# A state space block written as 16 steps a unit: most of the unit's side work put at other steps, a fifth product on GpSimd

## The reference, cut to what matters

```python
x = x + mamba(layernorm_over_channels(x))          # pixel_shuffle: sequence of 1 + 2304, width 128
t = tokens(x)
t = t + ffn(layernorm(t))                          # ffn keeps its input but for tokens 1..128
```

```python
u, z = split(seq @ in_proj.T); u = silu(conv4(u) + conv_b)
dt, B, C = split(u @ x_proj.T); dt = softplus(dt @ dt_proj.T + dt_b)
h[n] = exp(dt * A[n]) * h[n] + (dt * u) * B[n]      # a scan over time, for each state n
y = (sum_n h[n] * C[n] + u * D) * silu(z);  out = y @ out_proj.T
```

## Time and profile before

| | |
|---|---|
| median of 3 runs | 1246.59 us (1246.4 to 1247.64) |
| the profiled execution's own time | 1246.36 us |
| its span | 1244.6 us |
| granted TensorE clock, mean | 0.943 |
| busy | PE 86%, DVE 88%, POOL 82%, ACT 70% |
| units 1 to 20 | 972.7 us, 48.64 us each |

### The profile page before, as it was taken

The page is one execution under the profiler, slowest core; times in us unless marked ns, Lnnn a source line. Parts: engine busy times, 40 slices in busy tenths (PEclk is TensorE's granted clock), DMA queues, the critical chain, the costliest instruction groups (busy, mean ns, idle before and its releaser), DMA issues.

```text
span 1244.6 us, 13235 instructions
## 1 busy us (share of the span) xinstructions
PE 1064.5 (86%) x3786; PEld 635.6 (51%) x3786; DVE 1089.3 (88%) x1220; ACT 870.6 (70%) x1581; POOL 1024.0 (82%) x679
## 2 busy tenths in 40 slices
PE   6688998988898888989987988998899898887997
PEld 4345555555455455555554554554555455443454
DVE  2898999898999989999989899989899998878684
ACT  4687687676777775876767777758767767657653
POOL 4598988978889879889889798898898897858674
PEclk9899999899999999999989999989999989988899
DMA  7222223222222221222221322212222322334351
GB/s 179 93 102 78 84 83 104 83 84 86 75 103 77 90 95 68 87 99 85 83 104 57 103 84 84 103 59 108 78 84 83 103 80 90 102 115 164 107 179 28
DMA packets 64538, 116.79 MB, mean 94 GB/s; under 512 B 34218, under 2 KB 47954, under 8 KB 64466
## 3 DMA queue, kind: packets, MB, share of 16 engines
q1 hardware_dynamic: 64466, 115.96, 27.4%
HBM read 108.47 MB, written 7.47 MB: 93 GB/s over the span
## 4 chain that ended last, share of the span: by engine, by line
ACT 33%; PE 32%; DVE 23%; issue 10%; POOL 2%; DVEq 0%; DMA 0%; POOLq 0%; ACTq 0%; SPq 0%
PE Yp L785 15%; DVE SCAN L1111 13%; ACT DA L513 6%; DVE SCAN L1076 5%; PE PP L797 3%; PE PP L810 3%; PE PP L866 2%; ACT L541 2%; ACT L529 2%; ACT UDT L535 2%; DVE GATES L1157 2%; POOL SCAN L448 2%; DVE VV L1087 2%; ACT DAS L521 2%; PE PP L818 2%
## 5 line engine op out<-in xcount | busy, mean ns | idle before, releaser
L448 POOL TENSOR_TENSOR SCAN<-SCAN,CS 128x768 f32<-128x768 f32 x384 | 692.4, 1817 | 121.7 <-DVE SCAN L1111 120.6
L1111 DVE TENSOR_TENSOR_SCAN SCAN<-DA,CAR,SCAN 128x384 f32<-128x384 f32 x672 | 638.8, 1002 | 54.6 <-ACT DA L513 54.6
L785 PE MATMUL Yp<-SCAN,IDENT 128*128 128x384 f32 x1536 | 597.7, 516 | 72.4 <-DVE VV L1087 70.9
L513 ACT ACTIVATE DA<-UDT,A 128x384 f32<-128x384 f32 x672 | 377.9, 578 | 257.0 <-DVE SCAN L1111 256.9
L785 PEld LDWEIGHTS Yp<-SCAN,IDENT 128*128 128x128 f32 x1536 | 297.0, 201 | 260.4 <-POOL SCAN L448 89.3
L1076 DVE TENSOR_TENSOR SCAN<-UDT,BB 128x768 f32<-128x768 f32 x240 | 224.9, 937 | 19.8 <-PE BB L767 19.7
L456 POOL TENSOR_TENSOR SCAN<-UDT,BS 128x768 f32<-128x768 f32 x96 | 173.9, 1812 | 0.0
L926 PE MATMUL PP<-XN,WT 128*128 128x384 f32 x352 | 124.4, 486 | 1.4 <-ACT ZB L626 1.4
L767 PE MATMUL BB<-PT,SEL 96*128 96x384 bf16 x288 | 98.2, 341 | 7.4 <-DVE DA L1076 4.4
L926 PEld LDWEIGHTS PP<-XN,WT 128*128 128x128 f32 x352 | 66.6, 189 | 48.5 <-issue 1.9
L468 POOL TENSOR_TENSOR UDT<-UDT 128x768 f32<-128x768 f32 x23 | 41.7, 1814 | 52.7 <-DVE UDT L1161 52.7
(11 more groups left out here) (212 smaller groups left out, 1233.9 us busy)
## 6 DMA issues: line engine op xcount, KB each, us to landing
CS<-bc_rows SPq DMA_DIRECT2D x96, 768.0 KB, 4.0
BS<-bc_rows SPq DMA_DIRECT2D x24, 768.0 KB, 6.1
out<-XN SPq DMA_DIRECT2D x32, 192.0 KB, 2.5
X<-in_x SPq DMA_DIRECT2D x24, 192.0 KB, 3.6
X<-in_L_ffn_memory_tokens SPq DMA_DIRECT2D x16, 256.0 KB, 2.9
XN<-in_L_ffn_memory_tokens SPq DMA_DIRECT2D x16, 256.0 KB, 3.0
bc_rows<-XDT SPq DMA_DIRECT2D x24, 48.0 KB, 1.5
X<-in_L_ffn_memory_router SPq DMA_DIRECT2D x1, 512.0 KB, 4.3
```

Source lines behind the costliest of these rows:

```text
L448: pool.tensor_tensor(M[:, n1 % MRING], HB[:, n1 % HRING], over_halves(CS[:, n1 % CRING]), ALU.mult).then_inc(m_ready, 1)
L513: act.activation(DA[:, h, 0:T], DT[:, par, h], ACT.Exp, scale=A[:, h, n:n + 1])\
L785: last = pe.matmul(Yp[:, h, 0:T], IDENT[:, :], M[:, n3 % MRING, h], start=n3 == 0, stop=n3 == NS - 1)
L1111: dve.tensor_tensor_scan(HB[:, s % HRING, h], factor, term, CAR[:, ds(J * NS * HALVES + s * HALVES + h, 1)], ALU.mult, ALU.add).then_inc(s ...
```

## The change

No arithmetic changes. The product with B of state 11 goes from VectorE to GpSimd, `AHEAD` becomes states 14 and 15, whose factors are made at steps 10 and 11 of the same unit, and the side work is hung on other steps. With the steps on which the pieces stand on their main engines:

| piece | before | after |
|---|---|---|
| Silu of U and of z, with two table loads (ACT) | 0, for J+1 and J-1 | 13, for J+2 and J |
| x projection (PE), copies of its rows (ACT) | 3, 4, for J+1 | 14, 15, for J+2 |
| parts: `LESS` (PE) | 4, 5 | 15 (of the unit before), 0 |
| dt projection (PE), Abs and Relu (ACT) | 7, 7 | 2, 2 |
| rest of softplus (ACT), last two pieces (DVE) | 7 to 11, 12 | 3 to 10, 11 |
| `VV` (DVE) | 3 | 2 |
| output projection (PE), copy into X (ACT) | 4, 5 | 3, 4 |
| second norm: mean, variance (PE), `LNV2` (ACT) | 6, 9, 10 | 5, 7, 8 |
| D term (PE) | 10 | 4 |
| first norm: mean, variance (PE), `LNV` (ACT), GpSimd | 9, 11, 11, 15 | 4, 6, 7, 10 |
| z (PE), its copy (ACT) | 12, 12 | 8, 9 |
| convolution (PE) | 13, 14, 15 with 3, 3, 2 taps | 9 to 12 with 2 taps each |

The SP queue writes the rows of B and C of unit J+2 behind the last loads of unit J+1's first ones, and the load of `BS` now waits until GpSimd has used the products of the unit before. The routing moves from steps 8 to 14 to steps 3 to 9 of unit 21, and the tables of the mixing shift by up to one or two steps. In unit 0 the softplus stands two steps later (`late`).

```diff
-AHEAD = (1, 2)
+AHEAD = (14, 15)
-POOL_STATES = (3, 5, 7, 9)
+POOL_STATES = (3, 5, 7, 9, 11)
...
+            def copy_rows(u):
+                act.wait_ge(xp_ready, u + 1)
+                act.wait_ge(rows_written, 16 * u)
+                act.activation(XDT[XROW0:XROWS, :], PP[XROW0:XROWS, 1, 0:T], ACT.Copy)
+                act.wait_ge(parts_ready, u)
+                act.activation(PART[:, :], PP[0:DTROW, 1, 0:T], ACT.Copy).then_inc(hi_ready, 1)
...
+                if main and s == 13:
+                    act.preload_act_table_set("silu_and_others")
...
+                if conv and s == 15:
+                    copy_rows(c)
...
-                if front and s == 7:
+                if front and s == 2 + late(J):
                     act.wait_ge(dtp_ready, f + 1)
                     positive(act, dt_ready, f)
                     act.activation(SE[:, :, :], PPT, ACT.Abs).then_inc(sp_chain, 1)
                     act.activation(DT[:, fp], PPT, ACT.Relu).then_inc(relu_done, 1)
...
-                if back and s == 4:
+                if back and s == 3:
                     pe.wait_ge(v_ready, k + 1)
                     if front:
-                        pe.wait_ge(u_ready, f + 1)
+                        pe.wait_ge(relu_done, f)
...
-                if norm and s == 9:
+                if norm and s == 4:
...
-                if back and s == LAG:
+                if back and s == LAG - 1:
                     dve.wait_ge(ysum_done, NS * (k + 1))
...
-                if norm and s == 10:
+                if norm and s == 5:
                     dve.wait_ge(mean_ready, g + 1)
```

## The result

| | before | changed |
|---|---|---|
| median | 1246.49 us (4 runs) | 1372.48 us (1365.5 to 1376.63, 4 runs) |
| ratio of times | 1 | 1.1006, 95% interval [1.0948, 1.1063] |
| span of the profiled execution | 1244.6 us | 1374.4 us |
| units 1 to 20, each | 48.64 us | 54.62 us |

The change makes the kernel 10% slower. The sign was right; the change of 126 us is nearly twice the 66 us that were forecast (1313 us), and the time lies outside the range, which ended at 1345 us. All 20 middle units now take 54.6 us each, where before they took 47.4, 49.2 or 50.5 in turn.

A forecast was written before the change was run, and what follows sets the result against it. VectorE's work plus its waits on other engines bounds each unit: 43.85 + 6.6 + 0.6 + 0.9 = 51.95 us, times 20 = 1039; with the rest (about 272) and 1.8 us, 1313 us. Range 1255 to 1345 us.

The forecast's parts named there:

- The sign: Whole kernel: slower, given 0.85, against 0.02 for same and 0.13 for faster.
- The floor: VectorE's own work in a unit: falls from 44.7 to 43.85 us with one product with B less.
- The first, second and third place: VectorE's waits: `VV` 1.65 us; first norm's centring 2.5; state 8's factors 0.3 and state 12's spread 2.1; together 6.6.
- the second and the third place: TensorE queues: output projection through mean, ending at 17.7 us; z, a sum, two taps, then state 12's spread, ending at 33.6.
- Softplus on VectorE: Last softplus pieces beside a working GpSimd: 0.6 us more a unit, bounds minus 0.7 and plus 1.8.
- The clock: TensorE's slow spells after pauses: 0.9 us a unit, the old price scaled by shorter pauses; bounds nothing and 5.4.
- The third rival: TensorE's clock falls in two of three pauses in each unit: 54.65 us a unit, whole 1367 us; chance 10%.
- The rest of the span: Start, unit 0, units 21 to 23 and tail: left at 271.9 us, 10 us allowed either way.
- Faster, because the waits don't add up: Rival: VectorE's waits stay at 2.74 us, a unit takes 47.8, the whole 1230 us; chance 14%.

The follow-up runs named there:

- e5: Changed kernel with all four TensorE pauses of the unit filled with dummy matmuls (10, 7, 7 and 8): 1312.34 us.
- e1: Changed kernel with 12 dummy matmuls in each of two TensorE pauses, ahead of the first `LESS` and of the output projection: 1373.0 us.
- e10: Changed kernel with the product of state 11 back on VectorE, so four products on GpSimd: 1362.55 us.
- e12: Changed kernel with Relu first, dt u early, D term at 10, `LESS` later, `LNV2` first, convolution at 10 to 13, GpSimd's first norm at 12: 1187.39 us.
- e9: Kernel before with only the fifth product (state 11) moved to GpSimd, all steps as before: 1245.68 us.

## Why the prediction was wrong

*The floor.* One product less was taken as 0.85 us, and the floor of 43.85 us came out: VectorE's 45.3 us busy in the changed kernel, less the 1.5 us that softplus takes more.

*The first, second and third place.* `VV`, the centring and the product of state 12 are right in place, releaser and, at full clock, size. The factors were late at state 10 and not at state 8, so that their size agrees by luck. Together it is 6.2 us in e5 against 6.6. The terms named for the second and the third place add up to 0.2 and 0.3 us less than the times given for them, which changes nothing. The pause ahead of the spread for the next unit's state 0 was left out.

*Softplus on VectorE.* Right in kind, the term mis-sized: taken as 0.6 us, measured 2.50 + 1.57 - 1.64 - 0.96 = 1.5 us, inside the bounds given (-0.7 to 1.8). I let only the second piece wait longer than before. GpSimd was in hand at the start of the first one as well and at the start of the second.

*The clock.* This is the step that failed, by most. It was "0.9, the old price scaled by the shorter pauses", and it is 2.9 us a unit (changed kernel less e5): 1.3 of it in `VV`'s wait, 1.6 in that for the spread of state 6. The old price was a mean over units of which two in four had paid nothing and one, that of 50.5 us, had paid 3.1. I carried that mean over, as if each pause had a fixed chance. But here two of the pauses brought a spell in every one of the 20 units, both ahead of matmuls for which VectorE waits. The third rival, given 10%, names this, "two of three pauses in each unit". That its 54.65 us a unit meets the measured 54.62 is in part luck: its clock term of 3.6 is 0.7 too dear, its softplus term 0.9 too cheap, and the waits make up the rest.

*The rest of the span.* Left as it was, bound 10 us, and it is 282.0 against 271.9. The changed kernel reaches unit 1 at 97.2 in place of 86.1 us: unit 0, in which VectorE waits 4.3 us for the first norm's mean and 2.5 us for spreads, takes 50.3 in place of 43.3, and the start, in this execution, 4.1 more. The routing unit is 2.4 us longer and the one behind it 5.4 shorter.

In sum: 54.62 against 51.95 us a unit is 53.4 us (clock +2.0, softplus +0.9, the waits -0.4 and 0.2 unaccounted for, each a unit), the rest is 10.1, and 63.5 of the 63.6 us between 1313 and the profiled execution's 1376.63 are placed. *Faster, because the waits don't add up* fell; GpSimd's stop for dt u did go, and its going is what exposed softplus.

## What to carry to other kernels

When work is hung on steps by hand, ask of each piece not only when its input is there but what stands behind it in the same engine's list: here a Relu behind a pair of factors, and a mean behind a projection, cost more than a whole engine's product saved. A layout by hand from the rows finds such waits within half a microsecond; look for the pauses it leaves out as well. Don't carry a mean price of low clock from one order of work to another: a kernel that repeats itself can pay in each unit what the old one paid in a few, so price a spell at each pause behind which an engine waits, and measure the true price by filling all pauses at once. And when single mends each save more than their wait, look for the wait that falls in all of them before adding them up.

## What the runs showed of the hardware

- In the changed kernel, pauses of 2.0 to 3.0 us on TensorE are followed by a spell at 1.2 GHz in some places of the unit and not in others, and filling some of them moved the spells to others (e1) without changing the unit's 54.6 us; filling all four removed them (clock 1.00) for 2.9 us a unit. Three kernels (the changed one, e1, and e10 from its seventh middle unit on) settled on units of 54.6 us; why just there isn't shown.
- Two VectorE instructions that read both inputs from SBUF took 0.93 and 0.96 us beside a GpSimd that stood still, and up to 2.52 us each beside one at work. Where a GpSimd instruction was in hand when L1173 (L1157 before) started, it ended 0.82 us after that one: 609.35 to 610.17 us before, 738.27 to 739.09 in the changed kernel, 722.48 to 723.30 in e12. In the changed kernel GpSimd's own, queued at the same time, stretched from 1.81 to 2.52 and from 0.99 to 1.71 us. Products and scans with one input in PSUM took the same in all runs (0.92 to 0.96 and 0.98 to 1.02 us).
- The first scan of unit 0 starts at 43.6 to 47.2 us in the changed kernel and its variants, and at 42.8 and 46.4 in the kernel before and e9. No experiment here was about that.
